# Every third expert block of the middle segments moves its activation and its sum with the residual from ScalarE and GpSimd to VectorE

## The reference, cut to what matters

```
x = x + attn_a(layernorm(x))      # 16 heads, softmax over 512 keys, 40 features per head
x = x + ffn(layernorm(x))         # 8 experts, each row goes to the one with the largest gate
x = x + attn_b(layernorm(x))      # differential attention, 2 x 16 heads of 8 features, rotary
x = x + ffn(layernorm(x))
# ffn:
h = silu(x @ W1[e] + b1[e]);  o = h @ W2[e] + b2[e];  y = o * softmax(gate)[e]
```

## Time and profile before

| | us |
|---|---|
| median of 3 runs | 1520.86 (1516.44 to 1524.8) |
| the profiled execution | 1515.25 |
| its span, first to last instruction | 1513.4 |
| PE busy | 1382.8 (91%) |
| DVE busy | 1188.0 (78%) |
| ACT busy | 1070.1 (71%) |
| POOL busy | 678.6 (45%) |

### The profile page before, as it was taken

One profiled execution on the slowest core, in us unless ns is written; L12 is line 12 of the kernel. 1 busy time (PEld: TensorE's weight loads), 2 busy tenths in 40 slices (PEclk: granted clock), 3 DMA queues, 4 the chain that ended last, 5 costly groups with the idle time before them and its releaser, 6 DMA issues.

```text
span 1513.4 us, 26975 instructions
## 1 busy us (share of the span) xinstructions
PE 1382.8 (91%) x9162; PEld 594.7 (39%) x9162; DVE 1188.0 (78%) x2046; ACT 1070.1 (71%) x1958; POOL 678.6 (45%) x744
## 2 busy tenths in 40 slices
PE   7989899999999998999998889989899989998986
PEld 3323334344655332445542323223232234543475
DVE  6757788877777778786779799998997997778553
ACT  3566566676665676787787888887887876877822
POOL 5332334424422764387865643414433133964143
PEclk8999999999999999999999999999998997999999
DMA  3488676865772334555411542211111135643072
GB/s 80 122 268 248 192 213 192 258 203 169 232 203 61 95 119 136 183 160 166 138 39 36 159 138 85 64 43 54 54 49 36 44 93 171 182 146 95 24 245 85
DMA packets 125230, 199.81 MB, mean 132 GB/s; under 512 B 16728, under 2 KB 91186, under 8 KB 125094
## 3 DMA queue, kind: packets, MB, share of 16 engines
q1 hardware_dynamic: 115910, 184.23, 40.8%
q0 software_dynamic: 6016, 12.71, 2.4%
q10 hardware_dynamic: 3168, 1.15, 0.4%
HBM read 123.90 MB, written 72.59 MB: 130 GB/s over the span
## 4 chain that ended last, share of the span: by engine, by line
PE 66%; DVE 11%; ACT 11%; issue 5%; SPq 2%; POOL 2%; DMA 2%; ACTq 1%; another core or an unknown queue 0%; POOLq 0%; DVEq 0%
PE ps L1271 19%; PE ps L1259 11%; PE ps L1238 11%; DVE Mb L1587 9%; ACT P L1461 7%; PE ps L1367 6%; PE ps L1352 6%; PE ps L1204 3%; PE ps L1279 2%; PE ps L1220 1%; PE ps L1324 1%; PE ps L1305 1%; ACT OR L1468 1%; PE ps L1244 1%; PE ps L1344 1%
## 5 line engine op out<-in xcount | busy, mean ns | idle before, releaser
L1587 DVE TENSOR_REDUCE Mb<-ps 128x1 f32<-128x512 f32 (+1 forms) x1006 | 922.9, 966 | 167.4 <-PE ps L1238 159.6
L1461 ACT ACTIVATE P<-ps 128x512 f32<-128x512 f32 (+1 forms) x1273 | 797.9, 693 | 195.0 <-PE ps L1259 163.6
L1259 PE MATMUL ps<-STK 32*128 32x512 f16 (+1 forms) x1536 | 395.3, 388 | 34.6 <-ACT P L1461 20.2
L1271 PE MATMUL ps<-P,V 128*32 128x512 f32 x3072 | 409.4, 615 | 1.0 <-ACT OR L1468 0.2
L1238 PE MATMUL ps<-STK 32*128 32x512 f16 (+1 forms) x1536 | 375.4, 390 | 35.5 <-DVE Mb L1587 13.1
L1238 PEld LDWEIGHTS ps<-STK 32*128 32x128 f16 (+1 forms) x1536 | 100.8, 93 | 315.1 <-DVE Mb L1587 118.3
L1259 PEld LDWEIGHTS ps<-STK 32*128 32x128 f16 (+1 forms) x1536 | 106.6, 93 | 226.9 <-ACT P L1461 90.5
L1271 PEld LDWEIGHTS ps<-P,V 128*32 128x32 f32 x3072 | 64.9, 109 | 123.4 <-issue 111.6
L1861 POOL DMA_INDIRECT xs<-ROW,slot x64 | 64.0, 1000 | 103.7 <-DVE slot L1678 88.8
L1825 POOL CAST HL<-RT 128x512 f16<-128x512 f32 x47 | 28.7, 611 | 169.9 <-ACT RT L1407 149.1
L1352 PE MATMUL ps<-XT,WE 128*128 128x128 f32 x696 | 95.9, 284 | 5.1 <-ACT XT L1491 2.4
(11 more groups left out here) (160 smaller groups left out, 1374.9 us busy)
## 6 DMA issues: line engine op xcount, KB each, us to landing
WE<-wx SPq DMA_DIRECT2D x87, 576.0 KB
STK<-qka SPq DMA_DIRECT2D x56, 480.0 KB
qka<-HL SPq DMA_DIRECT2D x84, 256.0 KB, 4.2
STK<-qkb SPq DMA_DIRECT2D x64, 256.0 KB
qkb<-HL SPq DMA_DIRECT2D x96, 128.0 KB, 2.7
X<-xs SPq DMA_DIRECT2D x77, 129.5 KB
xs<-pad SPq DMA_DIRECT2D x8, 1036.0 KB
qka<-HL SPq DMA_DIRECT2D x42, 128.0 KB
```

The costliest lines, as they stand in the source:

```text
L1259: mm = eng.matmul(ps[:, bank + i, :], l_, r_, start=True, stop=True)
L1271: mm = eng.matmul(ps[32 * j:32 * j + 32, OB, :], V[:, b % 3, kt, at:at + 32], P[:, st % 3, j, :], start=(kt == 0 and (b >= B or hh % 2 == ...
L1461: eng.activation(P[:, st % 3, j:j + n, :], ps[:, bank:bank + n, :], ACT.Exp, scale=SCALE_A if g < 4 * B else SCALE_B).then_inc(sem("exp"), 1)
L1587: eng.tensor_reduce(Mb[:, g % 2, at:at + 4 * n - 3:4], ps[:, bank:bank + n, :], AX, ALU.max).then_inc(sem("mx"), 1)
```

## The change

Of the 46 blocks with the POOL form, those with m % 3 == 2 get the DVE form. These are 15 blocks: m = 20, 23, ..., 44 (nine of them, in segment 1) and m = 47, 50, ..., 62 (six, in segment 2). For each of them `silu_z`, `silu_p`, `weigh` and `plus_p` go, and `silu_b` and `combine` come. A second line adds a wait: before SP fetches new weights into a slot, the `plus_b2` of the block that used the slot must be done, beside its `down`.

```diff
 def on_pool(m):
 
-    return 0 < BLOCKS[m][0] < NS - 1 and not late(m)
+    return 0 < BLOCKS[m][0] < NS - 1 and not late(m) and m % 3 != 2
...
                 on.wait_ge("wst", 16 * (NE - 1))
                 if weight_before(m) is not None:
                     on.wait_ge("fo", weight_before(m) + 1)
+                    on.wait_ge("fbp" if on_pool(weight_before(m)) else "fb", nth(weight_before(m)))
```

## The result

The change made the kernel slower, by 1.1%. Its runs took 1535.95, 1537.94 and 1544.29 us against a median of 1522.83 us before (a fourth run, 2183 us at a mean clock of 0.55, was disturbed and is left out). The ratio is 1.0112, with a 95% interval of 1.0061 to 1.0163. Measured once more on another chip beside 23 runs of the kernel before (experiment 9), it was 1.0146 (1.0096 to 1.0197). The forecast was 1527 us, range 1511 to 1545: the sign and the range held, and the point was 11 us under the median of the three runs. A step of +6 us was forecast, and +15 us came.

The account below looks back on a forecast made before the run. PE was taken to bound the stretches with blocks, with DVE sharing the limit between them. The terms 0 + 0 + 0 + 6 gave +6 us, all at the end, added to the median for 1527 us; range 1511 to 1545 us.

Parts of the forecast that it names:

- PE sets the pace in the middle, DVE has room: Stretches with blocks: PE 94% and 95% busy, DVE 75% and 74%; added DVE work hidden, sum -0.1 us, taken as 0.
- The stall of `plus_b2`: Segments 1 and 2: with 15 of 46 POOL blocks gone, a third of its excess time goes, 3.0 and 2.5 us.
- SBUF operands: Added DVE instructions read one operand from PSUM, so keep 682 and 349 ns beside POOL; upper bound 11 us more on DVE.
- The end: Last `pv` to segment 3: groups moved ahead of the last gate make it later, 3.7 to 6.6 us, bound +9, taken +6.
- The waits in the row of score tiles: Last group: eleven score tiles with seven banks; PE waits for about four exponentials of 0.61 us, bounding the end at +9.
- The count of three `up` ahead of the last `pv`: End of attention: three `up` and three `down` of the moved groups were said to stand ahead of the last four `pv`.
- the count of six groups across the gate: Last gate to segment 3: five `up` and six `down` become two and three; six others, 6.6 us, stand ahead of the gate.
- The stretch without blocks: 800 to 1250 us: same work in a new order, taken as 0 with 5 us to either side.
- A: Middle: bunched `down` groups delay attention tiles 1.1 us each time, +16.5 us for fifteen blocks, 1543 us; chance 0.23.
- B: 5.5 us of stall and 6 us of chain share come back, the end costs only 3.7: 1513 us; chance 0.18.
- C: PE sets the pace in the middle, ACT's pace covers the moved work at the end: 1521 us, no change; chance 0.13.

Follow-up runs that it names:

- experiment 9: The change itself, unedited, measured once more on another chip beside 23 runs of the kernel before; 1.0146 against that kernel.
- Experiment 1: The change's 15 blocks get the DVE form, but all engines keep the order and banks of the kernel before; 1.000 against that kernel.
- 6: Against the kernel before, the 16 blocks with m % 3 == 1 get the DVE form instead of the change's 15, planned anew; 0.9967.
- 10: Kernel before with one planner number changed, the assumed cost of `plus_b2` 0.34 instead of 0.35, so a new order; 1.0015.
- 11: All 46 blocks get the DVE form, with order and banks of the kernel before; 1.0046 against that kernel.
- 12: The kernel with the 16 blocks m % 3 == 1 in DVE form, measured once more on another chip against the kernel before; 0.9986.
- 3: Only the nine blocks of segment 1 get the DVE form, planned anew; 1.0121 against the kernel before.
- 4: Only the six blocks of segment 2 get the DVE form, planned anew; 1.0072 against the kernel before.
- 8: Kernel before with one planner number changed, the assumed cost of `silu_p` on GpSimd 2.5 instead of 2.64, so a new order; 1.010.
- 2: All 46 blocks keep the POOL form, but tensor engine order and banks stand as planned for the change; 1.0303 against the kernel before.
- 7: The 15 blocks with m % 3 == 0 get the DVE form instead of the change's, planned anew; 1.0118 against the kernel before.
- experiment 5: The change, with the first product of blocks 66 to 76 allowed only behind the last `pv`; 1.0151 against the kernel before.

## Why the prediction was right, and where it was off

**PE sets the pace in the middle, DVE has room: right.** Experiment 1 has all of the added and removed work and is at 1.000. My sum for it was -0.1 us.

**The stall of `plus_b2`: right, and worth nothing.** 5.5 us were forecast, 6.3 measured; in experiment 1 its mean over the 46 blocks fell from 722 to 530 ns, and the time did not move. That is for both together, the shorter stall and the work that was added.

**SBUF operands.** The two added instructions kept 682 and 349 ns, so they did not contend with POOL.

**The end: right in kind and about in size.** The term was +6 us, bounds 3.7 and 9. From group 95 to the end the trace has 101.0 us against 90.9, +10.1. Of the low clock in these stretches, 19.1 us against 11.4, some 3 us are due (0.40 us each, see below). That leaves +7.0, and +6.4 in the trace of experiment 9. Across thirteen of the traces the last group takes 8.2 to 8.5 us where no expert group stands ahead of the last `pv` and scores alternate with `pv` (before, 1, 6, 10, 11, 12), 13.7 us with three `up` and three `down` (3, 4, 8), and 18.4 to 19.9 us with five and three and eleven score tiles in a row (the change, 2, 7, 9). Of the two costs that the term was made of, the moved groups are the large one: in the last group PE is busy for 9.2 us more than before and not busy for 0.9 us more. The waits in the row of score tiles are 1.07 us in the change, where up to four exponentials, 2.4 us, were allowed for. In experiment 5, with hardly any moved groups, they are 1.07 us again, and 0.69 us come ahead of the last `pv`. The count of three `up` ahead of the last `pv` was wrong (five), but not the count of six groups across the gate, on which the term rests.

**"The stretch without blocks: 0, with 5 us to either side": this step failed.** It measured +15.3 us in the first trace. Part is the order. Four traces have the new one (the change, 3, 5 and 9: 437.0, 431.0, 430.9, 430.0 us with 37.5, 20.5, 25.6 and 23.9 us at low clock) and four the old (before, 1, 4, 11: 421.7, 426.0, 422.6, 422.8 us with 10.2, 20.5, 10.2 and 13.7). Without 0.40 us for each us at low clock these are 422.0, 422.8, 420.7, 420.4 against 417.6, 417.8, 418.5, 417.3. So the order costs 3.7 us there, within my bounds, and the rest, some 11 us in this trace, is clock. Experiment 2, the fifth trace in which PE has the new order here, gives 422.7. Since the traces are of several chips, I also scaled each by its stretch up to group 34, which has one order in all of them; the difference is again 3.7 us. So the term of the sum was 0 where the order cost about 4, and what went beyond the bounds is a thing that the sum had no term for. From 836 to 849 us in the changed kernel the clock is down for 6.8 us, and DVE waits 6.0 us for tiles in two waits, the longer 3.8. The granted clock stands third from the right, 0.74:

```profile
836.00:849.00 13.00, 11.32 (x57) 3.68 (x53) 6.96 (x13) 8.45 (x16) 7.87 (x8) 0.74 0.26 73
```

**A term that was missing: the clock.** The runs of the change had a mean clock of 0.966 in the first measurement and 0.960 in the second. Those of before had 0.970 in the second; of the first only the clock of the profiled execution is known, 0.970 as well. In the second this is half of the 24 us. I had taken the clock of the profiled execution as given. Experiments 5, 7 and 2 lost clock as well (0.9625, 0.9623, 0.9590 against 0.970), experiments 6, 10 and 12 gained or kept it. Experiments 2, 5, 7 and 9 lie 0.008 to 0.011 below before, about three to five standard errors, and in all four PE has the order of the change in groups 92 to 94. That the order decides it is consistent with these runs, but what in an order does so stays open.

**Rivals.** A (bunching, 1543 us) is nearest to the measured time, but its mechanism did not come: the stretch of segment 1 grew by 3.4 us in the change and by 0.3 us in experiment 9 (about 2 us on average over the four traces with its order, corrected for clock and chip, where A asked for 10), segment 2 not at all at equal clock, and PE's share of the two is 92% and 92%, as over the same groups before (92% and 93%). Reductions that starve for good were seen in experiment 2 only. B (relief) is out by experiment 1, where the same relief with the same work gave nothing. C (nothing) was right for the work and wrong for the plan.

**Luck.** The forecast had the sign by its mechanism, the end. Its range held the time because it reached up to A's 1543 us, for a cause that did not come. The sum itself, +6 us of order cost, stands against 11.7 us at equal clock, and against 15 to 24 us with the clock that the runs got.

**What settles the cause:** new work in the old order costs nothing (1), the old work replanned can cost as much as the change (8), and the same amount of new work in another plan costs nothing again (6, 12). The change is slower because of the plan that follows from it: 6 to 7 us at the end, about 4 us in the stretch without blocks, about 2 us in segment 1, less 0.7 us in groups 92 to 94, and the rest by less granted clock. The first four are read from traces and add up to about the 11.7 us of experiment 9. None of them was taken away alone with success: experiment 5 tried it for the end, and the time did not come back.

## What to carry to other kernels

Where a planner orders all engines, a change of one cost or one engine is two changes; make the work change within the old order first, and replan the old work as a control. Look in the new order at the places where a fixed latency is covered by work that was kept for it: six groups moved across the last gate cost what they no longer cover. And compare runs at equal granted clock beside the plain times, or a plan's luck and the clock's can't be told apart.

## What the runs showed of the hardware

**The spread between runs of one kernel goes with the granted clock.** The 23 runs of before beside experiment 9 lie between 1502.2 and 1518.1 us, and their mean clocks between 0.977 and 0.965, with a slope of -1.20 us per 0.001 and a correlation of -0.98. On the three other chips the slope is -1.14, -1.22 and -1.23. At equal clock the mean of the runs of before has a standard error of 0.2 to 0.5 us, which is well under what the times alone tell (0.2 to 1.1 us for the kernels with 6 to 12 runs). A mean that is lower by 0.001 is 3.0 us at the lower level in 1513 us, so one us at 1.2 GHz costs 0.40 us. Some stretches of low clock lie in the middle of attention, with PE busy on both sides, and not in the same place in two runs. In the trace of before one goes from 1153.8 to 1164.0 us, and PE is busy for 18.3 of the 20 us ahead of it. The Trainium skill (TensorE: Matmul & The Clock Gate, its table of terms) takes the time at reduced clock times the share of clock that is missing as the penalty, which would be 0.5. The runs give 0.40. A likely reason, which no run shows, is that for part of that time PE isn't what is waited for.

**VectorE beside GpSimd.** `plus_b2`, with two operands in SBUF, took 722 ns on average in the middle before, 586 in the change, 530 in experiment 1 and 422 in experiment 11, as POOL's load fell, and 343 to 346 in segments 0 and 3, whose blocks have no multiplications on POOL. The order counts as well: with the multiplications of all 46 blocks still on POOL it took 624, 751 and 794 ns in experiments 2, 10 and 8. `silu_b`, with one operand in PSUM, took 680 to 683 ns in the mean of every trace.
